# Rotation tables gathered by GpSimd's indirect transfers, low halves of the exponentials on GpSimd, and another order of the bridge

## The reference, cut to what matters

```python
x = x + tanh(g_xattn[0]) * L0_xattn(layernorm(x), ctx, Wq, Wk, Wv, Wo)   # 16 heads of 96, keys from ctx and x
x = x + tanh(g_ffn[0])   * L0_ffn(layernorm(x), W_base, gate_W, A, B)    # 8 experts, top 2
x = x + tanh(g_xattn[1]) * L1_xattn(layernorm(x), ctx, ctx)              # linear attention, no weights
x = x + tanh(g_ffn[1])   * L1_ffn(layernorm(x), ...)                     # weight from Fourier coefficients
x = x + tanh(g_xattn[2]) * L2_xattn(layernorm(x), ctx, ctx, pos, mask, ...)
# in L2_xattn, for queries and keys alike
cos = cos_t[position_ids]; sin = sin_t[position_ids]      # tables of 512 rows x 128
q = q * cos + rotate_half(q) * sin
```

## Time and profile before

| | |
|---|---|
| median of 3 runs | 1708.32 us |
| the profiled execution's own time | 1710.52 us |
| its span, first to last instruction | 1708.4 us |
| TensorE busy | 1691.8 us, 99% of the span |
| VectorE, ScalarE, GpSimd busy | 1288.1, 875.1, 970.5 us |
| mean granted TensorE clock | 0.999 |
| moved by DMA | 69.45 MB, 41 GB/s |

### The profile page before, as it was taken

How to read it: one execution, slowest core, us unless ns; L and a number is a source line. 1 busy time by engine, 2 the same in 40 slices (tenths; PEclk the granted TensorE clock), 3 DMA queues, 4 the chain that set the end, 5 groups by cost and what they waited for, 6 DMA issues and landing times.

```text
span 1708.4 us, 27562 instructions
## 1 busy us (share of the span) xinstructions
PE 1691.8 (99%) x8818; PEld 1419.7 (83%) x8818; DVE 1288.1 (75%) x2382; ACT 875.1 (51%) x2445; POOL 970.5 (57%) x807
## 2 busy tenths in 40 slices
PE   9999999999999999999999999999999999999999
PEld 7888888786888888888888888888888888888887
DVE  7566566788887877777777788787777877777796
ACT  7656665654553545445454453454443545435451
POOL 3223241475685757657576574675665756657662
PEclk9999999999999999999999999999999999999999
DMA  6101010030210101101011110110110101101101
GB/s 219 32 14 38 13 35 7 23 106 13 63 38 25 49 20 54 37 25 49 18 55 37 31 48 27 31 56 25 43 37 25 51 23 49 37 25 49 38 13 50
DMA packets 37428, 69.45 MB, mean 41 GB/s; under 512 B 4426, under 2 KB 5194, under 8 KB 37234
## 3 DMA queue, kind: packets, MB, share of 16 engines
q1 hardware_dynamic: 36930, 67.83, 13.4%
q10 hardware_dynamic: 432, 0.79, 0.1%
HBM read 66.50 MB, written 2.10 MB: 40 GB/s over the span
## 4 chain that ended last, share of the span: by engine, by line
PE 90%; DVE 5%; ACT 2%; issue 1%; POOL 1%; DMA 0%; DVEq 0%; SPq 0%; ACTq 0%; POOLq 0%
PE ps L446 25%; PE ps L448 25%; PE ps L447 25%; PE ps L727 4%; PE ps L704 4%; PE ps L705 2%; PE ps L628 1%; PE ps L665 1%; ACT probs L2688 1%; PE ps L973 1%; DVE negmax L1605 1%; DVE ot_lo L1635 0%; DVE rope_b L1589 0%; POOL rope_a L3492 0%; DVE rope_b L1590 0%
## 5 line engine op out<-in xcount | busy, mean ns | idle before, releaser
L3510 POOL TENSOR_TENSOR probs<-probs,rsums 128x512 f32<-128x512 f32 (+1 forms) x160 | 194.5, 1216 | 260.1 <-DVE rsums L1625 258.9
L3492 POOL TENSOR_TENSOR rope_a<-rope_a,rope_b 128x512 f32<-128x512 f32 x160 | 207.0, 1293 | 225.2 <-DVE rope_b L1590 225.1
L2688 ACT ACTIVATE probs<-probs,negmax 128x128 f32<-128x128 f32 x512 | 199.9, 396 | 98.1 <-DVE negmax L1599 98.0
L446 PE MATMUL ps<-wo_hiL,ot_hi 128*128 128x512 f32 x608 | 244.1, 401 | 2.8 <-DVE ot_lo L1640 1.5
L446 PE MATMUL ps<-xt_hi,wq_hiL 128*128 128x512 f32 x608 | 243.3, 400 | 0.3 <-DVE xt_lo L1519 0.2
L448 PE MATMUL ps<-wo_hiL,ot_lo 128*128 128x512 f32 x608 | 237.8, 391 | 0.0
L448 PE MATMUL ps<-xt_hi,wq_loL 128*128 128x512 f32 x608 | 237.7, 391 | 0.0
L447 PE MATMUL ps<-wo_loL,ot_hi 128*128 128x512 f32 x608 | 237.2, 390 | 0.0
L447 PE MATMUL ps<-xt_lo,wq_hiL 128*128 128x512 f32 x608 | 236.7, 389 | 0.0
L2704 ACT CAST ot_hi<-ps 128x512 fp32r<-128x512 f32 (+1 forms) x160 | 90.3, 564 | 212.4 <-PE ps L448 210.8
L2697 ACT CAST pt_hiL<-ps 128x512 fp32r<-128x512 f32 (+1 forms) x160 | 107.6, 673 | 165.9 <-PE ps L727 106.9
(11 more groups left out here) (236 smaller groups left out, 4308.4 us busy)
## 6 DMA issues: line engine op xcount, KB each, us to landing
raw<-in_L_proj SPq DMA_DIRECT2D x108, 256.0 KB, 2.7
raw<-in_L_out SPq DMA_DIRECT2D x76, 256.0 KB, 2.7
raw<-in_F_w SPq DMA_DIRECT2D x16, 256.0 KB, 2.8
cn_raw<-in_ctx SPq DMA_DIRECT2D x8, 256.0 KB, 7.9
out<-x SPq DMA_DIRECT2D x8, 256.0 KB, 2.0
x<-in_x SPq DMA_DIRECT2D x7, 256.0 KB, 7.6
raw<-in_L_kv SPq DMA_DIRECT2D x6, 256.0 KB, 2.8
...
```

The lines of the kernel that those rows point to most:

```text
L446: pe.matmul(dst, l_hi, r_hi, start=start, stop=False)
L2688: e = act.activation(probs[:, row:row + L.keys], src, ACT.Exp, bias=offset[:, b % 2, h:h + 1], scale=L.scale, accum_out=sums[:, b % 2, h:h ...
L3492: gp.tensor_tensor(rope_a[:, a], rope_a[:, a], rope_b[:], ALU.add).then_inc(L.s_rsum, 1)
L3510: gp.tensor_tensor(pv, pv, rsums[:, b % 2].unsqueeze(2).to_broadcast([P, GH, L.keys]), ALU.mult).then_inc(L.s_p, 1)
```

## The change

The positions come as one column for each batch (128 x 8), and `positions` works on 8 columns. `table_rows(c)` on POOL issues two indirect transfers, one for each batch: 128 rows of 1 KB, cosine and sine side by side, from the table in HBM. The table splitting, the masks and their matmuls are gone. `rope_table(k)` is four PE transposes of 128 x 128. `e_tail` moves from DVE to POOL. `table_copy(k)` waits for its own table instead of all four. SP loses the table's load. All four `bridge` lists are in another order.

```diff
-        tab_raw = at("tab_raw", [P, C, 2, P], F32, r_wo)
-        tab_hi = at("tab_hi", [P, C, 2, P], F32R, r_wo + 4096)
-        tab_lo = at("tab_lo", [P, C, 2, P], F32R, r_wo + 8192)
-        pos_i = at("pos_i", [P, T], I32, r_k + 8192)
...
+        pos_i = at("pos_i", [P, B], I32, r_k)
...
+        tab = at("tab", [P, B, 2, P], F32, r_v + 4096)
...
-            sp.dma_start(pos_i[:], inp["pos"].broadcast_to([P, T])).then_inc(pos_in, 16)
+            sp.dma_start(pos_i[:], inp["pos"]).then_inc(pos_in, 16)
...
-            sp.dma_start(tab_raw[:], inp["rope2"]).then_inc(tab_in, 16)
...
             def rope_table(k):
-                t, tok = k // 2, slice(k % 2 * 512, (k % 2 + 1) * 512)
-                pe.wait_ge(tab_done, 1)
-                pe.wait_ge(oh, C)
+                t, h = k // 2, k % 2
+                pe.wait_ge(tab_in[h], 16 * HALF)
                 pe.wait_ge(f_x, 5 + k)
-                for c in range(C):
-                    pe.matmul(ps[:, 4 + k, :], tab_hi[:, c, t], onehot[c][:, tok], start=c == 0, stop=False)
-                    mm = pe.matmul(ps[:, 4 + k, :], tab_lo[:, c, t], onehot[c][:, tok], start=False, stop=c == C - 1)
+                for j in range(HALF):
+                    mm = pe.transpose(ps[:, 4 + k, j * P:(j + 1) * P], tab[:, h * HALF + j, t], ident)
                 mm.then_inc(oh_mm, 1)
...
+            def e_tail(b):
+                gp.wait_ge(a_head, b + 1)
+                gp.tensor_tensor(strip(xt_lo, b), probs[:, b % 2 * D:(b % 2 + 1) * D].rearrange("p (c t) -> p c t", c=C),
+                                 strip(xt_hi, b), ALU.subtract).then_inc(a_done, 1)
+
+            def table_rows(c):
+                if c == 0:
+                    gp.wait_ge(Lq[0].s_o, B * Lq[0].groups)
+                for b in (2 * c, 2 * c + 1):
+                    gp.indirect_dma_start(tab[:, b].rearrange("p t d -> p (t d)"), None, inp["rope2"],
+                                          bass.IndirectOffsetOnAxis(ap=pos_row[:, b:b + 1], axis=0)
+                                          ).then_inc(tab_in[b // HALF], 16)
```

More of the change, by code:

```diff
@@ L1316, in bridge @@
                 a0.transposes(6, last)
-                norm_transpose("F0", 2)
                 a0.out_proj(5, last)
                 a0.heads_out(6, last)
+                a0.transposes(7, last)
+                a0.out_proj(6, last)
+                norm_transpose("F0", 2)
                 norm_transpose("F0", 3)
+                a0.heads_out(7, last)
                 gates(0, 0)
-                a0.transposes(7, last)
                 gates(0, 1)
-                a0.out_proj(6, last)
-                a0.heads_out(7, last)
+                a0.out_proj(7, last)
                 norm_transpose("F0", 4)
@@ L1329, in bridge @@
                 norm_transpose("F0", 5)
-                a0.out_proj(7, last)
+                norm_transpose("F0", 6)
                 gates(0, 4)
@@ L1407, in bridge @@
                 a2.begin(3, 1)
+                norm_transpose("A2", 4)
                 a2.begin(4, 0)
-                norm_transpose("A2", 4)
                 a2.begin(5, 1)
@@ L2291, in bridge @@
                 a0.row_sum(1, last)
-                a0.evacuate(1, 0, last)
                 a0.ot_tail(0, last)
@@ L2325, in bridge @@
                 a0.pt_tail(5, last)
+                a0.residual(4, last)
+                a0.row_sum(6, last)
                 norm_tail("F0", 0)
[L2327 to L2328 removed]
                 a0.next_stats(4, last)
```

423 lines of the change are left out of this document (202 added, 221 removed).

## The result

The changed kernel took 1713.89 us (median of 7 runs, 1713.57 to 1715.55), the kernel before, beside it, 1708.53 (7 runs, 1708.21 to 1710.37). The ratio is 1.003, 95% interval 1.0021 to 1.0039: slower, by 5.4 us, beyond the 0.2% that can be told. Forecast were 1709.3 and a range to 1713.5, so the forecast's case was wrong, and the range missed by 0.4 us.

The account below looks back on a forecast made before the run. It took TensorE to bound most of the bridge, with VectorE nearly a second bound in 410 to 430. Terms -6.1 + 0.7 + 3.2 + 3.2 = +1.0 us gave a median of 1709.3 us, range 1702.2 to 1713.5.

Parts of the forecast that it names:

- the forecast's case: Whole kernel: the terms' sum holds, median 1709.3 us, own range 1706.5 to 1711.5; chance 0.38.
- Table matmuls: Linear attention, TensorE: four tables by transposes instead of matmuls save 6.1 us where TensorE was never idle.
- Linear attention: Gaps on TensorE at spread_out and numerators without the table matmuls as cover: +3.2 us, bounds 0 and 4.5.
- rival B: TensorE's gaps at batches 6 and 7 and numerators(1) lower its clock, 1.7 us per spell: 1711.0 or 1712.7; chance 0.27.
- VectorE's order in batch 2: Last group: the key's low half, moved between values' halves, delays TensorE's projection: +0.7 us, between 0 and 1.3.
- Batches 6 and 7: TensorE's new order there idles for probabilities, starts out_proj of batch 7 later, leaves work owed: +3.2 us, lower bound 1.5.
- Gathers: Eight gathers on GpSimd, each holding it at most 1.90 us, fit its idle time: 0.
- Low halves on GpSimd: 8 x 0.77 us leave VectorE, 8 x 1.30 us come to GpSimd: put at 0.
- Rival C: GpSimd is late with low halves behind gathers and norm_rstd: 4.2 us if none hidden, 1713.5; chance 0.10.
- Rival A: The 6.1 us saving stands since TensorE's gaps shorten elsewhere: 1702.2, or up to 1704.9; chance 0.25.

Follow-up runs that it names:

- e9: Kernel before with only the first 2 of each table's 8 matmuls, nothing else changed: 1708.54 us, ratio 0.9998.
- e10: e6 with a plain transfer of 128 rows on GpSimd's queue in place of each indirect one: 1709.04 us, ratio 0.9999.
- e8: Changed kernel with 9 more matmuls, results unread, in TensorE's gaps of the linear attention: 1711.86 us, 2.0 less than the changed kernel.
- e1: Kernel before's lists with the tables' part alone (gathers, transposes, no masks), low halves still on VectorE: 1712.51 us, ratio 1.0024.
- e6: e1 with two gathers moved behind the last norm_rstd of L0's feed-forward network: 1712.12 us, ratio 1.0021.
- e2: e1 with the low halves of the exponentials on GpSimd: 1713.19 us, ratio 1.0020.
- b1: Kernel before's lists up to the sixth experts, six gathers behind L0's last norm_rstd, low halves on GpSimd, linear attention rewritten: 1721.59 us, ratio 1.0076.
- c4: e1 with two gathers behind the linear attention's norm_rstd of batch 3, products(1, 0) and norm_transpose of batch 1 ahead of spread_out(4): 1714.0 us.
- c5: c4 with the last experts behind spread_out(0), and numerator_share(0) and attend(0) ahead of the last residual: 1715.65 us, ratio 1.0037.
- e5: Changed kernel's lists up to about 366 us, e1's lists behind: 1714.35 us, ratio 1.0034.
- c1: Kernel before with the changed kernel's four lists up to the gates of batch 5 (about 366 us): 1722.8 us, ratio 1.0079.

## Why the prediction was wrong

Three steps of the sum failed, all to the same side. The clock was put at nothing and took 2.0 us. `residual(0)` on VectorE had no term at all and cost 1.2. The linear attention's term was 0.7 to 1.0 too small. Part by part:

**Table matmuls, -6.1.** The instructions went as said (four blocks of transposes, TensorE 4.2 us less busy), but as a gain the term was too large by itself, not only with the new order. e9 gives 1.2 of 5.5 us at the full clock, none in the median, and e10, with the transposes in the old order, 1.3 of 6.1. With the linear attention's +3.2 beside it the forecast counted on 2.9. I had read "busy in 20.00 of 20 us" as "each microsecond of TensorE's own work is one of the kernel's time". Next to it stood VectorE at 18.19 of 20, which I called nearly a second bound, and then did not use as one.

**Linear attention, +3.2.** Mechanism right, the five places right, size low: 6.1 + 0.1 from the second turn on, less e8's 2.0, leaves 4.2, and e8's rows give 3.9. Two sizes were off: `numerators(1)` has 1.50 instead of 1.1, and `spread_out(1)` has 0.43, which I had not seen. My chain of the earlier trace rows left out `weight_sum(3)` (417.30 to 417.99), which stands ahead of the first share, and an exponential on ScalarE (416.02 to 416.83), behind which its copy of the first `spread_out` comes.

**The clock, 0 in the forecast, rival B.** This is the step that failed by most: 2.0 us by e8, and all seven runs of the changed kernel had a mean clock under 1. B named two places and 1.7 us for a spell. At the first, batches 6 and 7, the clock held; at the second, `numerators(1)`, it fell for longer than a spell at 304. What I had held against B is that 320 to 360 keeps its clock in spite of gaps. There TensorE's longest wait is 0.40 us (at 329.67).

**VectorE's order in batch 2, +0.7** (0 to 1.3): 1.9 by the table. I priced the key's low half alone, and the step that it bears on came as forecast: 0.7 from `out_proj(1)` to `out_proj(2)`. The larger part, +1.2 by `out_proj(1)`, is `residual(0)` behind the maxima and their stretched scaling: TensorE waits 0.99 us for it. I had not followed that move, nor GpSimd's.

**Batches 6 and 7, +3.2**: 5.6 - 1.9 = 3.7 by the trace, with the gaps where forecast: 1.40 us for the probabilities, `out_proj(6)` at 358.11 for 358.05, `out_proj(7)` at 365.56 for 365.38. The term stands.

**Gathers, 0** (bound 1.90 us each): in the changed kernel TensorE did not wait for them, so 0 came out, but by luck, since the bound was wrong: one holds GpSimd 3.1 to 4.2 us there, and in e1 and e6 that cost 2.70 and 2.05 us. The cover I named, GpSimd "free for 5.5 of 20 us", would not have held 6 x 3.2 = 19 us. What hides them, as far as e6 shows it, is that the new lists ask for GpSimd's `norm_rstd` late.

**Low halves on GpSimd, 0**: e2 against e1, no difference beyond the intervals. Rival C did not come: the one wait that the profile puts down to `xt_lo` was for `attend(0)`, as shown above. (e2 has such a row too, 1.01 us at `numerators(2)`; in e1, with the low halves on VectorE, the wait there is 1.01 us as well, and put down to `attend`.)

**The sum**: 1.9 + 3.7 - 6.1 + 4.2 + 2.0 = 5.7, against 5.4 measured. (The 4.2 is what is left of the trace's difference, so the sum closes by itself; only e8's 3.9 checks it.) Forecast: 0.7 + 3.2 - 6.1 + 3.2 = 1.0. Of the 4.7 between, 2.0 are the clock, 1.2 batches 1 and 2, 0.5 batches 6 and 7, 1.0 the linear attention. Rival A fell with e9 and e10: in the old order at most 1.3 of its 6.1 us arrive. b1, c4 and c5 found no order that gets more; that there is none is not shown.

**Open.** The front's size alone rests on the traces and on e5 against e10; c1 shows it only with clock loss on top. That rows of VectorE last until a row of GpSimd ends (1.12 and 4.42 us) is seen in the traces; why, and why only some do, was not tried. Nor do the runs say why the clock fell behind a wait of 1.38 us and not behind one of 1.40.
